# Routed expert results added into the stored residual by a scattering DMA, instead of gathered and combined at the end

## What is computed

```python
probs = softmax(h @ Wg)                      # h = layernorm(x)
vals, idx = top_k(probs, 2)                  # two of E = 8 experts for each token
weights = vals / (sum(vals) + EPS)
y_e = silu(h @ W1[e] + b1[e]) @ W2[e] + b2[e]
out = sum over the two chosen e of weights * y_e
out = out + 0.1 * (silu(h @ Ws1 + bs1) @ Ws2 + bs2)
x = x + tanh(g_ffn) * out
```

## Time and profile before

| | us |
|---|---|
| median of 3 runs (817.22, 821.48, 822.36) | 821.48 |
| the profiled execution, its own time | 812.57 |
| its span in the trace | 810.8 |
| PE busy (share of the span) | 681.3 (84%) |
| DVE busy | 544.4 (67%) |
| ACT busy | 435.0 (54%) |
| POOL busy | 469.3 (58%) |

### The profile page before, as it was taken

The page is one execution under the profiler, slowest core; times in us unless marked ns, Lnnn a source line. Parts: engine busy times, 40 slices in busy tenths (PEclk is TensorE's granted clock), DMA queues, the critical chain, the costliest instruction groups (busy, mean ns, idle before and its releaser), DMA issues.

```text
span 810.8 us, 20629 instructions
## 1 busy us (share of the span) xinstructions
PE 681.3 (84%) x7762; PEld 599.5 (74%) x7762; DVE 544.4 (67%) x1315; ACT 435.0 (54%) x835; POOL 469.3 (58%) x487
## 2 busy tenths in 40 slices
PE   1778999999999999999999976877672699999960
PEld 1567888888888888888888765767562599999860
DVE  5656887888888888888888845666455244444426
ACT  2545767676666666676767642443240354445425
POOL 4564777777767676777777633345446155545540
PEclk9999999999999999999999995978886799999995
DMA  5152000000000000000000004001105222222229
GB/s 184 48 176 69 5 8 5 9 6 5 8 6 8 6 8 5 8 6 8 5 5 2 3 2 72 27 31 39 36 30 89 57 76 73 74 63 76 70 63 292
DMA packets 43854, 35.75 MB, mean 44 GB/s; under 512 B 5376, under 2 KB 37904, under 8 KB 43760
## 3 DMA queue, kind: packets, MB, share of 16 engines
q1 hardware_dynamic: 34912, 19.33, 9.0%
q0 software_dynamic: 4720, 9.89, 3.9%
q10 hardware_dynamic: 4128, 5.25, 2.4%
HBM read 21.04 MB, written 13.42 MB: 42 GB/s over the span
## 4 chain that ended last, share of the span: by engine, by line
PE 64%; DVE 11%; ACT 9%; issue 4%; another core or an unknown queue 4%; POOL 3%; DMA 2%; ACTq 1%; SPq 1%; DVEq 0%; POOLq 0%
PE ps L972 8%; PE ps L1076 8%; PE ps L922 8%; PE ps L893 7%; PE ps L876 5%; PE ps L878 5%; PE ps L877 5%; PE ps L985 4%; ACT spo L382 4%; PE ps L956 4%; ACT prob L389 4%; PE ps L1062 3%; PE ps L1064 3%; PE ps L1063 2%
## 5 line engine op out<-in xcount | busy, mean ns | idle before, releaser
L510 POOL TENSOR_TENSOR rstd<-var_eps,expo 128x16 f32<-128x16 f32 x64 | 186.3, 2911 | 5.0
L358 ACT ACTIVATE qk_T<-ps,lnw 128x512 f32<-128x512 f32 x128 | 96.5, 785 | 59.5 <-PE ps L893 59.3
L553 POOL DMA_INDIRECT results<-spo,xs_ix x78 | 75.2, 964 | 82.0 <-DVE spo L856 67.0
L536 POOL DMA_INDIRECT routed<-w_raw,slot x64 | 62.0, 969 | 69.4 <-issue 51.7
L441 ACT ACTIVATE qk_T<-ps,b_cols 128x256 f32<-128x256 f32 x156 | 61.5, 475 | 70.5 <-PE ps L1064 69.8
L876 PE MATMUL ps<-w_hi,xc_hi 128*128 128x512 f32 x192 | 91.9, 479 | 1.2 <-DVE prob L643 1.2
L664 DVE TENSOR_TENSOR wide<-ps,rstd 128x512 f32<-128x512 f32 x128 | 84.5, 683 | 8.9 <-POOL rstd L510 8.9
L893 PE MATMUL ps<-ident,wide 128*128 128x128 f32 x512 | 74.4, 279 | 12.5 <-DVE xc_lo L580 12.0
L508 POOL TENSOR_TENSOR var_eps<-ss,eps 128x16 f32<-128x16 f32 x64 | 14.0, 219 | 117.6 <-DVE ss L630 117.6
L630 DVE TENSOR_REDUCE ss<-wide 128x16 f32<-128x1024 f32 x64 | 77.4, 1210 | 4.5 <-ACT wide L366 3.3
L893 PEld LDWEIGHTS ps<-ident,wide 128*128 128x128 f32 x512 | 62.7, 145 | 23.0 <-issue 10.0
(11 more groups left out here) (169 smaller groups left out, 1524.6 us busy)
## 6 DMA issues: line engine op xcount, KB each, us to landing
v_sb<-routed SPq DMA_DIRECT2D x39, 129.0 KB
c_in<-in_ctx SPq DMA_DIRECT2D x32, 64.0 KB, 1.8
w_raw<-in_L_ffn_W ACTq DMA_DIRECT2D x1, 2048.0 KB, 8.5
wide<-results SPq DMA_DIRECT2D x8, 256.0 KB, 4.8
w_raw<-results SPq DMA_DIRECT2D x8, 256.0 KB, 4.8
out_x<-x_res SPq DMA_DIRECT2D x8, 256.0 KB, 4.1
results<-spo,xs_ix POOLq DMA_INDIRECT x78
routed<-w_raw,slot POOLq DMA_INDIRECT x64
```

The lines of the kernel that those rows point to most:

```text
L358: nc.scalar.activation(qk_T[:, n, 4 * j:4 * j + 4, :].rearrange("p a n -> p (a n)"), ps[6 + j][:, :], ACT.Identity, bias=lnw[:, 2 * n + 1: ...
L510: nc.gpsimd.tensor_tensor(rstd[:, n, :], var_eps[:, n, :], expo[:, n, :], ALU.pow).then_inc(rstd_ready, 1)
L553: gp_.indirect_dma_start(out=results[:, :], out_offset=bass.IndirectOffsetOnAxis(ap=xs_ix[:, b4, a:a + 1], axis=0), in_=yb[:, b4, a, :], i ...
```

## The change

Five edits belong together.

1. `results` is gone. The output tensor gets spare rows at its end for the padding, and the 129th number of a row is now the token's own row in the output, the same for both choices. Each row of `routed` gets a 130th number, column `D + 1`: the token's weight for that choice.
2. SP stores groups 0 to 6 of `x_res` to the output as soon as `shared_out` is done with them, and POOL stores group 7 after its last routing scatter, then waits until all eight stores have landed.
3. DVE writes the biased result to `y_raw` and multiplies it by the row's weight out of `xs_in` into `yb`. So the slot of `xs_in` is in use until `r_yb`, on which SP now waits too.
4. POOL's scatters add into the output (`compute_op=ALU.add`). The two results of one token come under two experts, so two scatters may meet in one output row only if their experts differ. Every tile waits for the tile two before to have landed. Tiles 1 to 4 wait for the tile before. From tile 5 on POOL reads from the schedule a number that is 32 where the expert changes and 0 elsewhere, and waits for the tile before if it is 32.
5. Stage 4 is left out: the kernel ends when all scatters and stores have landed.

```diff
-ROW = D + 1
+ROW = D + 2
+PADS = (E + SPARE) * SUB
...
+        y_raw = wide[:, 0, 0:2 * RT].rearrange("p (u a n) -> p u a n", u=2, a=SUB)
...
-        results = nc.dram_tensor("results", [2 * TOKENS + PADS * P, D], F32, kind="Internal").ap()
...
+            for g in range(GROUPS - 1):
+                sp.wait_ge(f_x2, 2 * g + 2)
+                sp.dma_start(out_v[:, GT * g:GT * (g + 1), :], x_res[:, GT * g:GT * (g + 1), :]).then_inc(o_stored, 16)
 
             sp.wait_ge(pad_ready, 2)
...
                 if n >= 4:
                     sp.wait_ge(r_t, n - 3)
                     sp.wait_ge(r_ix, n - 3)
+                    sp.wait_ge(r_yb, n - 3)
...
             for k in range(4):
                 sp.wait_ge(r_sent[k], 16 * SUB * len(range(k, NT, 4)))
-            res_v = results[0:2 * TOKENS, :].rearrange("(c t p) d -> p c t d", c=2, p=P)
-            for g in range(GROUPS):
-                for c in range(2):
-                    sp.dma_start(y_in[g][:, c, :, :], res_v[:, c, GT * g:GT * g + GT, :]).then_inc(o_in[g], 16)
-            for g in range(GROUPS):
-                sp.wait_ge(o_b, g + 1)
-                sp.dma_start(out_v[:, GT * g:GT * (g + 1), :], x_res[:, GT * g:GT * (g + 1), :]).then_inc(o_stored, 16)
-            sp.wait_ge(o_stored, 16 * GROUPS)
+            sp.wait_ge(o_stored, 16 * (GROUPS - 1))
+            sp.wait_ge(o_last, 16)
...
-            for g in range(GROUPS):
-                sc.wait_ge(o_in[g], 32)
-                for j in range(GT):
-                    t = GT * g + j
-                    nc.scalar.activation(y_in[g][:, 1, j, :], y_in[g][:, 1, j, :], ACT.Copy, scale=wtok[:, t, 1:2]).then_inc(o_w, 1)
...
-            nc.gpsimd.iota(tok_i[:, :, :], pattern=[[TOKENS, 2], [P, TILES]], base=0, channel_multiplier=1).then_inc(expo_ready, 1)
+            nc.gpsimd.iota(tok_i[:, :, :], pattern=[[0, 2], [P, TILES]], base=0, channel_multiplier=1).then_inc(expo_ready, 1)
...
+            gp_.wait_ge(f_x2, 2 * GROUPS)
+            gp_.dma_start(out_v[:, TILES - GT:TILES, :], x_res[:, TILES - GT:TILES, :]).then_inc(o_last, 16)
+            gp_.wait_ge(o_stored, 16 * (GROUPS - 1))
+            gp_.wait_ge(o_last, 16)
+            gp_.wait_ge(sched_ready, 1)
             for n in range(NT):
                 b4, _ = r_slot(n)
                 gp_.wait_ge(r_yb, n + 1)
+                if n >= 2:
+                    gp_.wait_ge(r_sent[(n - 2) % 4], 16 * SUB * ((n - 2) // 4 + 1))
+                if 1 <= n <= 4:
+                    gp_.wait_ge(r_sent[n - 1], 16 * SUB)
+                elif n > 4:
+                    other = gp_.value_load(sched_i[0:1, 2, n:n + 1], min_val=0, max_val=16 * SUB)
+                    wait_apart(gp_, r_sent[(n - 1) % 4], other + 16 * SUB * ((n - 1) // 4))
                 for a in range(SUB):
-                    gp_.indirect_dma_start(out=results[:, :], out_offset=bass.IndirectOffsetOnAxis(ap=xs_ix[:, b4, a:a + 1], axis=0),
-                                           in_=yb[:, b4, a, :], in_offset=None).then_inc(r_sent[b4], 16)
+                    gp_.indirect_dma_start(out=out[:, :], out_offset=bass.IndirectOffsetOnAxis(ap=xs_ix[:, b4, a:a + 1], axis=0),
+                                           in_=yb[:, b4, a, :], in_offset=None, compute_op=ALU.add).then_inc(r_sent[b4], 16)
...
+                nc.vector.tensor_copy(rows[:, par, :, :, D + 1], wt.rearrange("p j c -> p c j")).then_inc(f_row, 1)
...
+            link(nc.vector.tensor_tensor(sched[:, 2, 1:NT], sched[:, 0, 1:NT], sched[:, 0, 0:NT - 1], ALU.not_equal))
+            link(nc.vector.tensor_scalar(sched[:, 2, 1:NT], sched[:, 2, 1:NT], 16.0 * SUB, None, ALU.mult))
...
-                nc.vector.tensor_tensor(yb[:, b4, :, :], ps[4 + n % 2][:, 0:SUB * D].rearrange("p (a n) -> p a n", a=SUB),
-                                        b2_all[:, bass.ds(expert, 1), :].to_broadcast([P, SUB, D]), ALU.add).then_inc(r_yb, 1)
-
-            for g in range(GROUPS):
-                ve.wait_ge(o_in[g], 32)
...
+                nc.vector.tensor_tensor(y_raw[:, n % 2, :, :], ps[4 + n % 2][:, 0:SUB * D].rearrange("p (a n) -> p a n", a=SUB),
+                                        b2_all[:, bass.ds(expert, 1), :].to_broadcast([P, SUB, D]), ALU.add).then_inc(r_raw, 1)
+                ve.wait_ge(r_raw, n + 1)
+                nc.vector.tensor_tensor(yb[:, b4, :, :], y_raw[:, n % 2, :, :], xs_in[:, b4, :, D + 1:D + 2].to_broadcast([P, SUB, D]),
+                                        ALU.mult).then_inc(r_yb, 1)
```

More of the change, by code:

```diff
@@ L41, in flamingo_block @@
     ctx_v = ctx.rearrange("b s d -> (b s) d").rearrange("(t p) d -> p t d", p=P)
-    out_v = out.rearrange("b s d -> (b s) d").rearrange("(t p) d -> p t d", p=P)
+    out_v = out[0:TOKENS, :].rearrange("(t p) d -> p t d", p=P)
     with ExitStack() as stack:
@@ L166, in flamingo_block @@
         yb = o_T[:, :, :, :].rearrange("p a b n -> p (a b n)")[:, 0:4 * SUB * D].rearrange("p (k a n) -> p k a n", k=4, a=SUB)
-        y_in = [a[:, 0:4 * 2 * GN].rearrange("p (u c j n) -> p u c j n", u=4, c=2, j=GT)[:, u, :, :, :]
-                for a in (wide[:, :, :].rearrange("p a n -> p (a n)"), w1_raw[:, :, :].rearrange("p e n -> p (e n)")) for u in range(4)]
+        y_raw = wide[:, 0, 0:2 * RT].rearrange("p (u a n) -> p u a n", u=2, a=SUB)
         ps = [bank(f"ps{i}") for i in range(8)]
@@ L208, in flamingo_block @@
         r_sent = [sem(f"r_sent{k}") for k in range(4)]
-        o_in, o_a, o_b = [sem(f"o_in{g}") for g in range(GROUPS)], sem("o_a"), sem("o_b")
-        o_w = sem("o_w")
-        o_stored = sem("o_stored")
+        r_raw = sem("r_raw")
+        o_stored, o_last = sem("o_stored"), sem("o_last")
         routed = nc.dram_tensor("routed", [E * REGION + SPARE * RT, ROW], F32, kind="Internal").ap()
-        results = nc.dram_tensor("results", [2 * TOKENS + PADS * P, D], F32, kind="Internal").ap()
         block = stack.enter_context(nc.Block())
@@ L531, in group @@
             def group(g, par, last):
-                wait_apart(gp_, f_slot, g + 1, (f_row, 3 * g + 3))
+                wait_apart(gp_, f_slot, g + 1, (f_row, 4 * g + 4))
                 for c in range(2):
@@ L855, in _ @@
                 ve.wait_ge(r_y, n + 1)
-                nc.vector.tensor_tensor(yb[:, b4, :, :], ps[4 + n % 2][:, 0:SUB * D].rearrange("p (a n) -> p a n", a=SUB),
-                                        b2_all[:, bass.ds(expert, 1), :].to_broadcast([P, SUB, D]), ALU.add).then_inc(r_yb, 1)
-            for g in range(GROUPS):
-                ve.wait_ge(o_in[g], 32)
-                for j in range(GT):
-                    t = GT * g + j
-                    nc.vector.scalar_tensor_tensor(x_res[:, t, :], y_in[g][:, 0, j, :], wtok[:, t, 0:1], x_res[:, t, :],
-                                                   ALU.mult, ALU.add).then_inc(o_a, 1)
-                ve.wait_ge(o_a, GT * g + GT)
-                ve.wait_ge(o_w, GT * g + GT)
-                nc.vector.tensor_tensor(x_res[:, GT * g:GT * g + GT, :], x_res[:, GT * g:GT * g + GT, :], y_in[g][:, 1, :, :],
-                                        ALU.add).then_inc(o_b, 1)
+                nc.vector.tensor_tensor(y_raw[:, n % 2, :, :], ps[4 + n % 2][:, 0:SUB * D].rearrange("p (a n) -> p a n", a=SUB),
[3 more added lines that the diff above has]
+                                        ALU.mult).then_inc(r_yb, 1)
         @block.tensor
@@ L1071, in row_out @@
                 if n >= 2:
-                    pe.wait_ge(r_yb, n - 1)
+                    pe.wait_ge(r_raw, n - 1)
                 w2e = w2_sb[:, bass.ds(expert, 1), :, :].rearrange("p a c n -> p (a c) n")
@@ L1113 @@
         args.append(nc.dram_tensor(f"in_{name}", a.shape, mybir.dt.from_np(a.dtype), kind="ExternalInput").ap())
-    args.append(nc.dram_tensor("out_x", [B, S, D], F32, kind="ExternalOutput").ap())
+    args.append(nc.dram_tensor("out_x", [TOKENS + PADS * P, D], F32, kind="ExternalOutput").ap())
     flamingo_block(nc, *args)
     r = run_bass_kernel_spmd(nc, [arrays], core_ids=[0])
-    return r.results[0]["out_x"]
+    return np.asarray(r.results[0]["out_x"])[0:TOKENS].reshape(B, S, D)
```

11 lines of the change are left out of this document (5 added, 6 removed).

## The result

The changed kernel takes 830.31 us (828.46 to 832.47, 4 runs), the kernel before 821.82 (817.22 to 822.36, 4 runs) in the same session: ratio 1.0131, interval 1.0082 to 1.018. It is slower by 1.3%, where the prediction said 801.4 us and faster. The time lies in the range, next to the case "POOL becomes the bound", which stood at 833.7 us with a chance of 0.14.

A forecast was written before the change was run, and what follows sets the result against it. PE was taken to bound the row tiles, DMA and DVE what follows. 810.8 - 23.0 + 0.3 + 2.3 + 0.3 = 790.7, a gain of 20.1; from the median 821.48, 801.4 us. Forecast's own range 793 to 806, the whole up to 834.

The forecast's parts named there:

- POOL becomes the bound: Rival: adding scatters hold POOL 1.5 us, a tile takes 4.05 us, nothing is won back; 833.7 us, chance 0.14.
- s: Time of one adding scatter on POOL: taken as 0.96 us like the plain one, bounds 0.96 and 1.9.
- turning point, 1.34: Time in us of one adding scatter on POOL from which the predicted gain is gone.
- L + 0.2 - 0.75 = 1.65: Cost in us of each of POOL's 11 waits for the landing of the tile before.
- 24 us can be won and 18 are asked: POOL over 39 tiles: some 0.6 us won back in each, against 11 waits; level again at the end.
- L: Landing of an adding scatter behind its issue on POOL: taken as 2.2 us, bounds 1.27 and 3.6.
- g: On POOL, from readiness to a tile's first scatter, schedule read included: taken as 0.75 us, bounds 0.6 and 1.2.
- The end: Behind the row tiles: tail removed, -23.0 us; last landing 2.3 us later; end of program adds about 0.3.
- DVE's multiplication: Extra DVE step in each row tile: 0.45 us with semaphore, hidden in 1.18 us idle; only the last tile pays.
- the schedule's two links: Ahead of the row tiles: two more links of about 0.2 us, taken at nothing under 8 us of cover.
- The landing: Rival: waiting for the tile two before bounds the row tiles; gain gone at 3.85 us, 830 us, chance 0.08.
- DVE was late: Rival: addition and multiplication overrun DVE's idle 1.18 us and put 15 us into PE's ring; 816 us, chance 0.04.

The follow-up runs named there:

- the kernel with three tiles unsent: Kernel with plain scatters to rows of their own and no waits between scatters, its last three tiles computed but not scattered: 795.31 us, ratio 0.9814.
- the kernel that mixes them: Kernel with adding scatters, own rows and no waits, changed so odd tiles overwrite and every other pair of tiles sends 64 of 128 rows: 757.07 us, one execution.

## Why the prediction was wrong

- **The step that failed: "s ... I take 0.96, the nearest row".** An adding scatter holds POOL 1.56 us (median). The bounds of 0.96 and 1.9 held it; the choice within them did not. "Since rows and indices are the same" is true and says nothing of the addition. By the prediction's own turning point, 1.34, the sign was decided here, and with a tile at 3.72 of 3.63 us nothing is won back between waits. With the addition taken off and all waits kept, the kernel is 1.7% faster than before, so it is this term that turned the sign. The rival's mechanism was right: POOL became the bound. That its last landing, 822, was near the measured 824.3 is luck: it took 4.05 us for a tile where 3.72 were measured, 12.5 us too much over 38 tiles, and 1.65 for a wait where 2.6 were, 10.5 too little. That its time, 833.7, is near the median of 830.3 is luck too, since the sum set against profiles gives 823 where 827.9 was measured. Its reason, a cost for each row, was wrong: most of the extra is fixed.
- **"A wait costs about L + 0.2 - 0.75 = 1.65."** Measured 2.6 to 2.8. The 0.2 behind a landing is 0.77. And the subtraction of 0.75 assumed that a tile that doesn't wait pays the schedule's read; it pays 0.30, since the read runs beside the scatter before. Between the tiles' last and next scatter a wait leaves 1.85 + 0.77, of which 0.30 would be there anyhow: 2.3, and 2.6 with the longer landings (3.72 and 5.30 us occur).
- **"24 us can be won and 18 are asked."** Both terms failed, for the reasons above: almost nothing could be won, and about 29 were asked.
- **L right.** 3.4 us from issue to landing less 1.56 is 1.85, predicted 2.2 within 1.27 to 3.6. The plain one is 2.2 - 0.96 = 1.24. The Trainium skill, DMA: Bandwidth & Descriptors (Latency and other measured facts), has about 800 ns as the least round trip of a DMA to HBM. Adding one such trip to the plain landing, as the prediction's estimate did, gives too much: the difference between the two is 0.6.
- **g wrong in both states.** Predicted were 0.75, within 0.6 and 1.2. Where POOL is behind, it is 0.30, since the read runs beside the scatter before. Where POOL waits for its results, the kernel with plain scatters and all waits shows it, in DVE's and POOL's rows for one tile:

```profile
678.29 0.42 DVE L864 TENSOR_TENSOR spo<-wide,v_sb 128x256 f32<-128x256 f32 x1
```

```profile
680.12 0.96 POOL L555 DMA_INDIRECT out_x<-spo,xs_ix  x1 [1.28 <-DMA out_x<-spo,xs_ix]
```

  From 678.71 to 680.12 are 1.41 us, and ten tiles of this kernel that have nothing else to wait for have 1.39 to 1.41; without read and waits it is 0.28. (The row names a landing, but in some of the ten the scatter starts before the tile before has landed.) It decided nothing, because POOL keeps the pace of the tiles either way. The read itself shows 0.29 us in most tiles of the changed kernel and 0.50 at most, and 0.15 for its checks. The Trainium skill, same page and section, puts such a read at about 600 ns at least; these rows decide against it.
- **The end wrong.** "About 0.3" behind the last landing is 3.6 us. The tail's removal was right, all 23.0, but it had covered POOL's closing stretch. So the forecast would have been too high with plain scatters too. With them and without waits the gain was 12.6 us in the medians of one session, not 20.1. In the profiles it was 15.4, across two sessions: 23.0, less 6.1 behind the landing, less 1.5 for a later last landing.
- **Right as costed, where it could be seen:** DVE's multiplication takes

```profile
670.09 0.17 DVE L839 COPY xs_ix<-v_sb 128x2 int32<-128x2 int32 x1 [2.92 <-DMA out_x<-spo,xs_ix]
670.23 0.42 DVE L861 TENSOR_TENSOR wide<-ps,b_all 128x256 f32<-128x256 f32 x1
670.69 0.42 DVE L864 TENSOR_TENSOR spo<-wide,v_sb 128x256 f32<-128x256 f32 x1
```

  0.42 us like the addition ahead of it, and in the kernel with plain scatters and no waits the tiles keep 3.53 us, against 3.52 before. In the last session they didn't keep their pace with it (4.03 us on average in the kernel with three tiles unsent). Whether it would have cost in the first session, POOL hides. These rows also show the lag: the index copy has waited 2.92 us for a landing, and everything follows at once. The last group's store (0.82 us on POOL at 628.62, landed in 2.8) is in long before the first scatter. Of the rows for the weights and the schedule's two links nothing is seen in the first session, where the first scatter comes 0.3 us later; in the second it came 3.4 us later, and kernels that carry the same edits had it anywhere from 608.7 to 616.3, against 610.6 before. So no cost is shown, and none excluded.
- **The other rivals.** The landing did not become the bound: at 3.4 us from issue it is far from it, and the constant wait is free. In the changed kernel DVE was late only because POOL was. The change does what it says.

## What to carry to other kernels

Where an engine that has slack takes over an operation that the trace doesn't show, compare its slack with the upper bound of the price: here POOL idled 1.41 to 1.46 us a tile, of which 0.30 stay between any two scatters; of the 1.1 left the addition asked 1.2. Waits are free only while their engine has slack; the same 11 waits cost nothing beside plain scatters and 31 us beside adding ones, so two edits that are each harmless must be costed together. And a tail that is taken away may have covered something: ask what the program still has to do behind the engine that now ends last.

## What the runs showed of the hardware

- An indirect scatter of 128 rows of 512 bytes holds POOL 0.96 us plain and 1.56 adding. In the kernel that mixes them it is 0.98 and 1.59 with 128 rows, 0.93 and 1.45 with 64. Both leave 0.30 before the next. The adding one lands 3.4 us after its issue, the plain one 2.2.
- After a landing for which it waits, POOL starts its next scatter 0.7 to 0.8 us later, against 0.30 back to back. A register read ahead of a scatter hides under the one before; where POOL waits for its results, read and checks put 1.40 us between result and scatter instead of 0.28.
- A program that ends on POOL's DMA ends 7.4 us after the end of the last plain scatter on POOL and 5.5 after the last adding one. In that time the profile shows POOL's queue in its closing DRAIN, which ends 6.7 to 7.2 us after a last plain scatter and 5.2 to 5.5 after an adding one. Why it takes that long it doesn't show.
- The same kernel took 772, 810 and 822 us in three sessions, with the row tiles' stage 136.4 us long in the profile of the 772 us session and 143.4 in that of the 822, while a stage bound by POOL took 179.3 and 179.6. Most of the rest, 31.9 us, is time ahead of the row tiles that the trace puts down to another core or an unknown queue.
